# Routing the attention tiles beside attention instead of after it

## The chip, the cores and the metric

The kernel runs on one core of one Trainium2 chip. Its engines are TensorE (PE), VectorE (DVE), ScalarE (ACT), GpSimd (POOL) and SyncE (SP); DMA transfers run on 16 DMA engines and are issued here by SyncE and GpSimd, after the change by ScalarE too. The metric is the device time of one execution in microseconds.

## The reference

For 32 sequences of 256 tokens (D = 128) an attention layer with residual, then four layers of a mixture of experts with residual. Top 2 of 4 experts are chosen for each token by a router; the layers act on u, the normed output of the attention part.

```
x  = x + layernorm(linear_attention(layernorm(x)))     # 16 heads, causal, relu(q), relu(k)
u  = layernorm(x)
for l in range(4):
    logits = u @ router_w[l] + router_b[l]             # top 2 experts, gates from their softmax
    xhat   = normalised u
    expert e: u + gelu((xhat*g[e]+b[e]) @ w1[l,e] + b1[l,e]) @ w2[l,e] + b2[l,e]
    u = gate-weighted sum over the two chosen experts
x  = x + layernorm(u)
```

## The kernel before

The program is two blocks. In the first, attention works on 16 tiles of 512 tokens (`NT`), with x of all tiles in SBUF as `x1`. Each engine runs a `body(t)`, in a hardware loop for the middle tiles. In a body, VectorE masks scores, divides, and takes statistics three times: of x of tile t+1 (`x_stats`), of the projected output of tile t-1 (`o_stats`) and of x1 of tile t-1 (`x1_stats`). For each of the three GpSimd computes the reciprocal deviation (`rstd`: ve, then rs), and VectorE norms with it (`x_norm`, `make_x1`, `make_u`). TensorE transposes the normed xn into `ps_a`, projects to q, k and v, and makes scores and numerators. ScalarE empties PSUM (`evacuate`: xnT, qT, kT, ktok, vx, den) and copies the projection (`copy_o`). `make_u` writes u of all tiles into one SBUF tensor.

SyncE issues in order: x of tile 0, wqkv and wo, the other x tiles one after another, the small parameters, w1, then the zeroing of the two DRAM buffers `regions` (49 transfers each, from a tile `zero`), and then x1 of each tile into the output.

The second block begins with routing the 16 tiles (`for r in range(NT)` on each engine). For a tile, TensorE transposes u (`start_transposes`) and multiplies by the routers of all four layers (`start_logits`); VectorE chooses the two experts (`choose`), finds the gate's argument (`difference`) and, from counts that TensorE sums (`count`), each token's place in the region of its pair of experts (`place`); ScalarE computes the tanh of the gate and copies u into the row; GpSimd writes gates and identity and sends the rows out in four indirect DMAs (`rows_out`). There are two row buffers (`nrow`). Meanwhile w1 and w2 of layer 0 are split into a high and a low part (`split_w1`, `split_w2`) and stored. When all tiles are placed, VectorE makes a table of expert tiles (`table_counts`, `table_tiles`), SyncE stores the biases and loads the first rows (`rows_in`), and the experts' steady loop over 84 tiles runs (`N`).

Of the kernel before, what the change touches and what calls it, by code (L numbers as in the profile page):

```python
# [4 lines left out]
F32 = mybir.dt.float32  # L27
F32R = mybir.dt.float32r
# [41 lines left out]
ZEROS = 49  # L70


def sandwich_kernel(nc, x, wqkv, wo, router_w, router_b, ln_g, ln_b, w1, b1, w2, b2, out):
    ctx = ExitStack()
    with ctx:
# [7 lines left out]
        u = sb("u", [P, NT * TILE])  # L83
# [5 lines left out]
        cs = sb("cs", [P, L * E])  # L89
        rb = sb("rb", [P, L * E])  # L90
        onesf = sb("onesf", [P, P])
# [4 lines left out]
        slot, ones_nb = sb("slot", [P, NB]), sb("ones_nb", [P, NB])  # L96
# [5 lines left out]
        regions = [nc.dram_tensor(f"regions{q}", [ROWS, W], F32).ap() for q in range(2)]  # L102

# [7 lines left out]
        s_regions = sem("regions_zero")  # L111
# [24 lines left out]
        out_t = out.rearrange("(t s) n d -> t (s n) d", t=NT).rearrange("t (b p) d -> t p b d", p=P)  # L136

# [5 lines left out]
        with att:  # L143
# [32 lines left out]
            blank = asb("blank", [P, P])  # L176
            numbers = [asb(f"numbers{n}", [P, n], I32) for n in (NB, CL, NTL)]
# [6 lines left out]
            b1_rows = qx[0]  # L184

# [8 lines left out]
            def _(sp):  # L194
# [4 lines left out]
                with sp.Fori(1, NT) as t:  # L199
                    sp.wait_ge(s_x, t * 16)  # L200
                    sp.dma_start(blocks(x1[:, ds(t * TILE, TILE)]), x_t[ds(t, 1)].rearrange("o p b d -> p (o b) d")).then_inc(s_x, 16)
# [4 lines left out]
                sp.dma_start(rw[:].rearrange("h (l e) -> h l e", l=L), router_w.rearrange("l h e -> h l e")).then_inc(s_small, 16)  # L206
                sp.dma_start(rb[:], router_b.rearrange("l e -> (l e)").partition_broadcast(P)).then_inc(s_small, 16)
# [10 lines left out]
                with sp.Fori(0, NT) as t:  # L218
                    sp.wait_ge(a_x1, t + 1)
                    sp.dma_start(out_t[ds(t, 1)].rearrange("o p b d -> p (o b) d"), blocks(x1[:, ds(t * TILE, TILE)])).then_inc(s_prefill, 16)  # L220
# [3 lines left out]
            def _(pool):  # L224
# [8 lines left out]
                g.memset(onesf[:], 1.0)  # L233
# [23 lines left out]
                with pool.Fori(0, 3 * NT) as n:  # L257
                    rstd(n)

                g.memset(upper[:], 0.0)  # L260
                g.memset(first_row[:], -BIG)
                g.memset(ones6[:], 1.0)
                g.memset(ones_nb[:], 1.0)
                g.memset(ones_b[:], 1.0)
                g.memset(blank[:], 1.0)
                g.iota(numbers[0][:], pattern=[[P, NB]], base=0, channel_multiplier=1)
                g.iota(numbers[1][:], pattern=[[TILE, CL]], base=0, channel_multiplier=0)
                g.iota(numbers[2][:], pattern=[[1, NTL]], base=0, channel_multiplier=0).then_inc(s_c0, 1)
                pool.wait_ge(s_c0, 1)
                g.affine_select(out=blank[:], in_=blank[:], compare_op=ALU.is_ge, fill=0.0, base=-1,  # L270
                                pattern=[[1, P]], channel_multiplier=-1).then_inc(s_c1, 1)
                for q, (e, f) in enumerate(PAIR_CLASSES):
                    c = slice(e * E + f, e * E + f + 1)
                    g.memset(upper[:, c], 1.0)
                    g.memset(class_row[:, q:q + 1], float(TILE + q * TOKENS))
                    g.memset(first_row[:, c], float(TILE + q * TOKENS) - BIG)
                    g.memset(of_class[:, 2, q:q + 1], float(e))
                    g.memset(of_class[:, 3, q:q + 1], float(f))
                g.tensor_copy(slot[:], numbers[0][:])
                g.tensor_copy(thresholds[:], numbers[1][:])  # L280
                g.tensor_copy(tiles[:], numbers[2][:])
                pool.wait_ge(s_c1, 1)
                g.tensor_copy(before[:], blank[:]).then_inc(s_consts, 1)
# [5 lines left out]
            def _(dve):  # L289
# [86 lines left out]
                def make_u(t, n):  # L376
                    dve.wait_ge(a_rs, n + 1)
                    for b in range(NB):
                        last = normed(u[:, ds(t * TILE + b * P, P)], x1[:, ds(t * TILE + b * P, P)], b)
                    last.then_inc(a_u, 1)  # L380

                def body(t, par, prev, nxt, n):
# [27 lines left out]
                    reciprocal(t, 3)  # L410

# [13 lines left out]
                with dve.Fori(1, NT // 2 - 1) as q:  # L425
                    body(q * 2, 0, True, True, q * 6 - 1)
                    body(q * 2 + 1, 1, True, True, q * 6 + 2)
# [15 lines left out]
            def _(act):  # L443
                a = nc.scalar

                def copy_o(t):
                    act.wait_ge(a_o_ps, t + 1)
                    if not isinstance(t, int) or t > 0:
                        act.wait_ge(a_on, t)
                    a.activation(o_sb[:], ps_b[:], ACT.Identity).then_inc(a_o, 1)  # L450

# [29 lines left out]

                evacuate(0, 0)
                evacuate(1, 1)
                copy_o(0)
                evacuate(2, 0)
                copy_o(1)
                evacuate(3, 1)
                with act.Fori(2, NT // 2) as q:
                    copy_o(q * 2 - 2)
                    evacuate(q * 2, 0)  # L490
                    copy_o(q * 2 - 1)
                    evacuate(q * 2 + 1, 1)
                copy_o(NT - 2)
                act.wait_ge(s_cols_ps, 1)
                a.activation(cols[:], ps_a[:, 0:112], ACT.Identity).then_inc(s_cols, 1)
                a.activation(cs[:], ps_a[:, P:P + L * E], ACT.Identity)
                copy_o(NT - 1)
                for l in range(L):
                    act.wait_ge(s_b1rows_ps, l + 1)
                    a.activation(b1_rows[:, l, :], ps_b1[l][:], ACT.Identity).then_inc(s_b1rows, 1)  # L500

            @block.tensor
            def _(pe):
# [5 lines left out]
                def transposes(t):  # L509
                    pe.wait_ge(a_xn, t + 1)  # L510
                    if not isinstance(t, int) or t > 0:
                        pe.wait_ge(a_den, t)
                    for b in range(NB):
                        last = nc.tensor.transpose(ps_a[:, blk(b)], xn[:, blk(b)], ident[:])
                    last.then_inc(a_xT_ps, 1)

# [84 lines left out]
                def body(t, par, prev, nxt):  # L601
                    scores(t, par, 0, not prev)
                    scores(t, par, 1, not prev)
                    if prev:
# [20 lines left out]
                with pe.Fori(1, NT // 2 - 1) as q:  # L625
# [5 lines left out]
                pe.wait_ge(s_small, 6 * 16)  # L631
                pe.wait_ge(a_den, NT)
                nc.tensor.transpose(ps_a[:, 0:112], rows[:], ident[0:112, 0:112])
                mm(ps_a[:, P:P + L * E], onesf[:], rw[:], start=True, stop=True).then_inc(s_cols_ps, 1)
                project(NT - 1)

# [12 lines left out]
                for l in range(L):  # L649
# [3 lines left out]
                    last.then_inc(s_b1_ps, 1)  # L653


        s_ir = sem("identity_router")

        z_uT_ps, z_uT, z_lu_ps, z_lu, z_u = (sem(f"z_{n}") for n in ("uT_psum", "uT", "logits_psum", "logits", "u_copied"))

        s_raw, s_wst, s_whigh, s_wrest = sem("raw_weights_in"), sem("split_weights_out"), sem("weights_high"), sem("weights_rest")  # L660
# [9 lines left out]
        t_id, t_valid, t_link, t_oh, t_nd, t_th, t_gate = (  # L670
            sem(f"t_{n}") for n in ("id", "valid", "chain", "class", "difference", "tanh", "gates"))
        t_cnt, t_pos, t_row, t_base, t_tab = (sem(f"t_{n}") for n in ("counts_psum", "position", "row", "base", "table"))
        s_scat = [sem(f"rows_out{q}") for q in range(2)]
# [3 lines left out]
        w1d = nc.dram_tensor("w1_split", [L, E, P, 2 * F], F32).ap()  # L677
        w2d = nc.dram_tensor("w2_split", [L, E, P, 2 * F], F32).ap()
# [3 lines left out]
        with exp:  # L682
# [9 lines left out]
            wr1, wr2 = esb("wr1", [P, F]), esb("wr2", [P, F])  # L692
            wst1, wst2 = esb("wst1", [P, 2 * F], F32R), esb("wst2", [P, 2 * F], F32R)
# [22 lines left out]
            base = esb("base", [P, CL])  # L716
            ir = esb("ir", [P, D + L * E])
# [18 lines left out]
            def wait(eng, signal, count):  # L736
                if count > 0:
                    eng.wait_ge(signal, count)

            def ps_c(r):  # L740
                return (ps_h[0] if r < NT else ps_q)[:, CNT].rearrange("p (b c) -> p b c", c=CL)
# [681 lines left out]
```

## Time and profile before

| what | value |
|---|---|
| time, median of 3 runs | 1749.76 us (1746.67 to 1753.34) |
| time of the profiled execution | 1748.56 us |
| its span | 1746.5 us |
| mean granted clock of TensorE | 0.933 of full speed |
| busy: PE, DVE, ACT, POOL | 86%, 74%, 70%, 50% |
| DMA moved | 323.96 MB |

The span is the profiled part of the execution. Shares are averages over attention, routing and experts, which have different limits, so they are to be read by stretches of time. SPq in a row is SyncE's queue: its time there is that of issuing a transfer, not of moving it.

### The profile page before, as it was taken

What the parts mean: (1) busy time and instruction counts of PE and PEld (TensorE: products, weight loads), DVE (VectorE), ACT (ScalarE), POOL (GpSimd) and SP (SyncE); (2) the same over time, 40 slices, a digit from 0 to 9 for tenths busy, and PEclk for the clock granted to TensorE, in tenths of its full rate; (3) what the DMA queues carried; (4) which work ended last, traced back from release to release, by engine and by line L of the source; (5) the groups of instructions that cost most, each with busy time, mean ns of one, the idle gap of its engine ahead of it and who ended that gap; (6) DMA issues with size and microseconds to landing.
All of it is one profiled execution on the core that took longest, in us unless ns stands there. A gap on an engine that the chain in (4) does not pass through costs nothing. (4 is left out here: it accounts for less than half of the span.)

```text
span 1746.5 us, 39659 instructions
## 1 busy us (share of the span) xinstructions
PE 1501.3 (86%) x11654; PEld 1179.6 (68%) x11654; DVE 1299.8 (74%) x4048; ACT 1231.0 (70%) x2137; POOL 875.5 (50%) x1434
## 2 busy tenths in 40 slices
PE   7899999843329999989999998999999898888882
PEld 4556655533227888878888887878888787766761
DVE  6989999833337888778888887888888787666662
ACT  4445444211139888878888887888888788999992
POOL 1111111155543555645555554555555457788776
PEclk9999999955559999999999999999999999999996
DMA  3899820012246667656676675567767556766651
GB/s 91 304 404 405 340 65 12 20 62 80 69 146 201 217 209 233 222 182 201 194 223 214 199 239 184 182 195 239 212 210 234 187 192 174 188 180 179 184 137 8
DMA packets 196044, 323.96 MB, mean 185 GB/s; under 512 B 47789, under 2 KB 127999, under 8 KB 195872
## 3 DMA queue, kind: packets, MB, share of 16 engines
q1 hardware_dynamic: 168608, 298.46, 52.0%
q0 software_dynamic: 27264, 23.54, 6.0%
q8 instruction: 67, 1.10, 0.3%
q14 instruction: 105, 0.86, 0.2%
HBM read 218.99 MB, written 108.71 MB: 188 GB/s over the span
## 5 line engine op out<-in xcount | busy, mean ns | idle before, releaser
L1071 DVE TENSOR_TENSOR hl<-hg,hh 128x1024 fp32r<-128x1024 f32 x336 | 409.2, 1221 | 221.1 <-ACT hh L996 221.1
L990 ACT ACTIVATE hg<-ps_h,bb 128x512 f32<-128x512 f32 x672 | 438.4, 684 | 136.2 <-PE ps_h L1343 133.6
L904 POOL DMA_INDIRECT regions<-nrow,posi x316 | 358.0, 1133 | 139.7 <-issue 76.8
L996 ACT ACTIVATE hh<-hg 128x1024 fp32r<-128x1024 f32 x336 | 355.2, 1057 | 2.8
L1341 PE MATMUL ps_h<-xTh,w1b 128*128 128x512 f32 x672 | 288.6, 429 | 2.1 <-DVE xTl L1087 1.4
L1343 PE MATMUL ps_h<-xTh,w1b 128*128 128x512 f32 x672 | 266.8, 397 | 0.0
L1342 PE MATMUL ps_h<-xTl,w1b 128*128 128x512 f32 x672 | 266.3, 396 | 0.0
L1358 PE MATMUL ps_y<-hh,w2b 128*128 128x512 f32 x672 | 266.1, 396 | 0.0
L1356 PE MATMUL ps_y<-hh,w2b 128*128 128x512 f32 x672 | 265.3, 395 | 0.0
L1357 PE MATMUL ps_y<-hl,w2b 128*128 128x512 f32 x672 | 264.6, 394 | 0.0
L1372 PE MATMUL ps_q<-ir,yb 128*128 128x140 f32 (+2 forms) x1008 | 152.8, 284 | 22.5 <-DVE nrow L1108 13.9
L1372 PEld LDWEIGHTS ps_q<-ir,yb 128*128 128x128 f32 x1008 | 134.9, 190 | 48.4 <-issue 23.7
L913 POOL DMA_INDIRECT out_dram<-fin,fidi x84 | 135.0, 1607 | 53.6 <-ACT fin L1008 31.6
L975 ACT ACTIVATE xh<-row,pnmr,prs 128x128 f32<-128x128 f32 x336 | 137.9, 487 | 20.9 <-POOL pnmr L858 20.8
L253 POOL TENSOR_TENSOR ve<-mv,epsc 128x4 f32<-128x4 f32 x48 | 9.6, 201 | 281.6 <-DVE mv L299 281.6
L1343 PEld LDWEIGHTS ps_h<-xTh,w1b 128*128 128x128 f32 x672 | 127.9, 190 | 28.9
L1357 PEld LDWEIGHTS ps_y<-hl,w2b 128*128 128x128 f32 x672 | 127.2, 189 | 29.2
L1356 PEld LDWEIGHTS ps_y<-hh,w2b 128*128 128x128 f32 x672 | 127.2, 189 | 28.6
L1358 PEld LDWEIGHTS ps_y<-hh,w2b 128*128 128x128 f32 x672 | 127.2, 189 | 28.3
L1341 PEld LDWEIGHTS ps_h<-xTh,w1b 128*128 128x128 f32 x672 | 128.4, 191 | 21.1 <-DVE xTl L1087 1.8
L1342 PEld LDWEIGHTS ps_h<-xTl,w1b 128*128 128x128 f32 x672 | 128.6, 191 | 18.4
L893 POOL TENSOR_SCALAR nrow<-th 128x4 f32<-128x4 f32 x79 | 15.6, 198 | 216.0 <-ACT th L961 215.9
(197 smaller groups left out, 2643.2 us busy)
## 6 DMA issues: line engine op xcount, KB each, us to landing
w1b<-w_split SPq DMA_DIRECT2D x168, 512.0 KB, 4.3
w2b<-w_split SPq DMA_DIRECT2D x168, 512.0 KB, 4.2
regions<-zero SPq DMA_DIRECT2D x98, 582.0 KB, 12.8
row<-regions SPq DMA_DIRECT2D x84, 294.0 KB, 4.4
w_split<-wst SPq DMA_DIRECT2D x32, 512.0 KB, 5.2
wr<-in_L_ffn_w_dram SPq DMA_DIRECT2D x32, 256.0 KB, 4.6
regions<-nrow,posi POOLq DMA_INDIRECT x316, 3.0
x<-in_L_attn_x_dram SPq DMA_DIRECT2D x16, 256.0 KB, 2.9
```

The costliest lines, as they stand in the source:

```text
L904: g.indirect_dma_start(out=regions[layer % 2], out_offset=bass.IndirectOffsetOnAxis(ap=posi[r % 2][:, b:b + 1], axis=0), in_=nrow[r % 2][: ...
L975: last = a.activation(xh[:, blk(b)], row[n % ROWBUFS][:, b, 0:D], ACT.Identity, scale=rs[:, b:b + 1], bias=nmr[:, b:b + 1])
L990: a.activation(hg[c // 2 % PAIRS][:, c % 2 * TILE:(c % 2 + 1) * TILE], ps_h[c % BANKS][:], ACT.Gelu, bias=bb[n % 4][k // FC][:, k % FC:k % ...
L996: a.activation(hh[j % PAIRS][:], hg[j % PAIRS][:], ACT.Identity).then_inc(hi, 1)
L1071: v.tensor_tensor(hl[n][:], hg[n][:], hh[n][:].bitcast(F32), ALU.subtract).then_inc(lo, 1)
L1341: mm(o[:], w[:, high], xTh[n % 2][:], start=True, stop=False)
L1342: mm(o[:], w[:, high], xTl[n % 2][:], start=False, stop=False)
L1343: mm(o[:], w[:, low], xTh[n % 2][:], start=False, stop=True).then_inc(s1, 1)
L1356: mm(y[:], w[:, high], hh[j][:, h], start=k % FC == 0, stop=False)
L1357: mm(y[:], w[:, high], hl[j][:, h], start=False, stop=False)
L1358: last = mm(y[:], w[:, low], hh[j][:, h], start=False, stop=k % FC == FC - 1)
L1372: last = mm(o, yb[m % 2][e][:, blk(b)], ir[:, 0:width(m)], start=True, stop=True)
```

## The change

Routing of the attention tiles moves into the first block, tile t-2 in body t. `make_u` writes u straight into one of four row buffers (`arow`). TensorE transposes the row's u (`rows_T`), and multiplies it by the routers and sums the counts (`logits_and_counts`), in `ps_a`; ScalarE empties these and computes the tanh. GpSimd takes over `choose` and `place`, with instructions linked by a semaphore, and sends the rows out between its `rstd`s. Zeroing is issued by ScalarE as 14 transfers (7 zeroing steps in each) before its first `evacuate`. The split of layer 0's weights goes to the ends of bodies 4, 6, 8 and 10, and its loads and stores to SyncE's list. The hardware loops of attention are written out. The second block no longer routes; it begins with the tables and the biases.

```diff
@@ sync, block 1: router and small parameters ahead of x; zeroing gone; weights of layer 0
+                raw_weights(0)
...
-                sp.wait_ge(s_pool0, 1)
-                for q in range(2):
-                    flat = regions[q].rearrange("r w -> (r w)").rearrange("(z p n) -> z p n", z=ZEROS, p=P)
-                    for n in range(ZEROS):
-                        sp.dma_start(flat[n], zero[:]).then_inc(s_regions, 16)
...
+                    g = split_in(t - 1)
+                    if g is not None:
+                        store_weights(g)
+                        if g + 1 < E:
+                            raw_weights(g + 1)
@@ gpsimd, block 1
+                def choose(m):
+
+                    q = arow[m % AROWS]
+                    pool.wait_ge(z_lu, m + 1)
+                    at = D + (L - 1) * E
+                    g.tensor_scalar(q[:, :, ID], slot[:], float(m * TILE), None, ALU.add).then_inc(t_id, 1)
+                    chained(g.tensor_tensor(a_lg[:], q[:, :, at:at + E], over_blocks(rb[:, 0:E]), ALU.add))
+                    link()
...
+                    g.tensor_tensor(a_nd[:], a_pd[:, :, 0], a_pd[:, :, 1], ALU.add).then_inc(t_nd, 1)
+                def place(m):
...
+                    chained(g.tensor_tensor(a_tq[:], counted[:, 0:NB, :], over_blocks(base[:]), ALU.add))
...
+                    g.tensor_scalar(a_posi[m % 2][:], a_posf[:], BIG, None, ALU.add).then_inc(t_row, 1)
...
+                rstd(0)
+                n = 1
+                for t in range(NT + 4):
+                    if t + 1 < NT:
+                        rstd(n)
+                        n += 1
+                    if t == 0:
+                        numbers_and_classes()
+                    if 0 <= t - 4 < NT:
+                        rows_out(t - 4, range(3))
+                    if 0 <= t - 1 < NT:
+                        rstd(n)
+                        n += 1
+                    if 0 <= t - 4 < NT:
+                        rows_out(t - 4, range(3, 4))
+                    if 0 <= t - 1 < NT:
+                        rstd(n)
+                        n += 1
+                    if 0 <= t - 3 < NT:
+                        place(t - 3)
+                    if 0 <= t - 2 < NT:
+                        choose(t - 2)
+                pool.wait_ge(s_regions[1], ZEROS // ZBATCH * 16)
+                for q in range(2):
+                    pool.wait_ge(s_scat[q], NT // 2 * NB * 16)
@@ vector, block 1
                     for b in range(NB):
-                        last = normed(u[:, ds(t * TILE + b * P, P)], x1[:, ds(t * TILE + b * P, P)], b)
+                        last = normed(arow[t % AROWS][:, b, 0:D], x1[:, ds(t * TILE + b * P, P)], b)
...
                     reciprocal(t, 3)
+                    if split_in(t) is not None:
+                        split(split_in(t))
@@ scalar, block 1
+                    rows_T(t)
...
+                        copy_o(t - 1)
+                    logits_and_counts(t)
+                    if t + 1 < NT:
+                        evacuate(t + 1, (t + 1) % 2)
+                    if split_in(t) is not None:
+                        split(split_in(t))
...
+                act.wait_ge(s_pool0, 1)
+                for q in range(2):
+                    flat = regions[q].rearrange("r w -> (r w)").rearrange("(y z p n) -> y p z n", y=ZEROS // ZBATCH, z=ZBATCH, p=P)
+                    for y in range(ZEROS // ZBATCH):
+                        a.dma_start(flat[y], zero[:].unsqueeze(1).to_broadcast([P, ZBATCH, zero.shape[-1]])).then_inc(s_regions[q], 16)
                 evacuate(0, 0)
@@ tensor, block 1: body(t)
+                    if t >= 2:
+                        rows_T(t)
                     if prev:
                         project(t - 1)
                     numerator(t, par, 0, not prev)
+                    logits_and_counts(t)
                     scores(t, par, 2, False)
                     if nxt:
                         transposes(t + 1)
@@ block 2: the loops over r in range(NT) are gone on all engines
```

## Rows read from the trace of the kernel before

**Rows 1.** The page's first line: span of the profiled execution.
```profile
span 1746.5 us, 39659 instructions
```
**Rows 2.** Busy time by stretches: stretch, length, engines, clock, DMA share, GB/s.
```profile
240.00:260.00 20.00, 18.49 (x342) 11.97 (x342) 18.92 (x57) 9.19 (x19) 3.64 (x6) 1.00 0.04 13
352.00:492.00 140.00, 49.45 (x272) 42.57 (x272) 49.63 (x243) 24.20 (x56) 74.48 (x125) 0.50 0.21 71
```
**Rows 3.** Timeline, GpSimd, routing: start, us, engine, line, operation [idle before <-releaser].
```profile
370.74 1.08 POOL L904 DMA_INDIRECT regions<-nrow,posi  x1 [0.80 <-POOL posi L898]
...
497.44 0.97 POOL L904 DMA_INDIRECT regions<-nrow,posi  x1 [0.30 <-issue]
498.72 0.97 POOL L904 DMA_INDIRECT regions<-nrow,posi  x1 [0.30 <-issue]
```
**Rows 4.** Timeline, VectorE and SyncE's queue, end of the routing stage.
```profile
489.00 0.74 DVE L1216 SCALAR_TENSOR_TENSOR wst<-wr,cols,wst 128x512 fp32r<-128x512 f32 x1
490.26 0.34 DVE L1165 TENSOR_TENSOR num<-base,first_row 128x3 f32<-128x3 f32 x3
...
494.71 0.20 DVE L1207 CAST tabi<-tabf 128x84 int32<-128x84 f32 x1
...
503.30 4.12 SPq L813 DMA_DIRECT2D row<-regions  x4
```
**Rows 5.** Timeline, SyncE's queue, attention.
```profile
56.00 154.68 SPq L217 DMA_DIRECT2D regions<-zero  x98
211.05 134.82 SPq L220 DMA_DIRECT2D out_dram<-x  x16
```
**Rows 6.** Line 217, the zeroing transfers: time of an issue, and to landing.
```profile
L217 SPq DMA_DIRECT2D regions<-zero x98: 332/1318/4249, 56.0 to 209.2; - x98
...
DMA to landing us min/median/max: 5.4/12.8/19.1
```
**Rows 7.** DMA traffic of the stretch from 60 to 215 us.
```profile
DMA packets 15772, 60.91 MB, mean 393 GB/s; under 512 B 1623, under 2 KB 2103, under 8 KB 15762
```
**Rows 8.** Timeline, ScalarE, start of the kernel and one tile.
```profile
9.07 0.60 ACT L459 ACTIVATE xnT<-ps_a 128x512 f32<-128x512 f32 x1 [7.00 <-PE ps_a L514]
...
241.96 0.69 ACT L480 ACTIVATE den<-ps_a,epsc 128x512 f32<-128x512 f32 x1 [3.97 <-DVE rec L334]
```
**Rows 9.** Timeline, GpSimd and VectorE, start of the kernel and end of attention.
```profile
2.69 0.11 POOL L234 MEMSET order<- 128x16 f32 x1
...
348.26 1.16 DVE L286 TENSOR_SCALAR u<-x,mv,rs 128x128 f32<-128x128 f32 x4 [1.41 <-POOL rs L255]
...
351.35 0.29 POOL L919 COPY ir<-ident 128x128 f32<-128x128 f32 x1 [0.35 <-POOLq L143]
```
**Rows 10.** Timeline, GpSimd, one tile of attention.
```profile
249.96 0.20 POOL L253 TENSOR_TENSOR ve<-mv,epsc 128x4 f32<-128x4 f32 x1 [4.54 <-DVE mv L299]
...
255.31 0.20 POOL L253 TENSOR_TENSOR ve<-mv,epsc 128x4 f32<-128x4 f32 x1 [4.06 <-DVE mv L299]
255.59 1.01 POOL L255 TENSOR_TENSOR rs<-ve,half 128x4 f32<-128x4 f32 x1
264.20 0.20 POOL L253 TENSOR_TENSOR ve<-mv,epsc 128x4 f32<-128x4 f32 x1 [7.60 <-DVE mv L299]
```
**Rows 11.** Timeline, VectorE and GpSimd, experts.
```profile
541.89 1.24 DVE L1071 TENSOR_TENSOR hl<-hg,hh 128x1024 fp32r<-128x1024 f32 x1 [1.01 <-ACT hh L996]
...
542.03 1.28 POOL L877 TENSOR_SCALAR valid<-slot,tabf 128x4 f32<-128x4 f32 x1
```
**Rows 12.** Timeline, VectorE, one tile of attention.
```profile
245.45 1.11 DVE L286 TENSOR_SCALAR xn<-x,mv,rs 128x128 f32 x4 [0.19 <-POOL rs L255]
...
256.33 1.26 DVE L322 TENSOR_TENSOR_SCAN cumk<-ones,kT 128x256 f32<-128x256 f32 x2
257.63 0.69 DVE L325 TENSOR_TENSOR qcumk<-qT,cumk 128x512 f32<-128x512 f32 x1
```
**Rows 13.** DMA issues: line, KB each, median us from issue to landing.
```profile
biases<-bst SPq DMA_DIRECT2D x1, 40.0 KB, 9.7
```

More of the change, by code:

```diff
@@ L110, in sandwich_kernel @@
         s_w1all = sem("w1_all_in")
-        s_regions = sem("regions_zero")
+        s_regions = [sem(f"regions_zero{q}") for q in range(2)]
+        s_router = sem("router_in")
+        s_raw, s_wst, s_whigh, s_wrest = sem("raw_weights_in"), sem("split_weights_out"), sem("weights_high"), sem("weights_rest")
+        z_uT_ps, z_uT, z_lu_ps, z_lu, z_cnt = (sem(f"z_{n}") for n in ("uT_psum", "uT", "logits_psum", "logits", "counts"))
+        z_pool = sem("z_chain")
+        t_id, t_valid, t_link, t_oh, t_nd, t_th, t_gate = (
+            sem(f"t_{n}") for n in ("id", "valid", "chain", "class", "difference", "tanh", "gates"))
+        t_cnt, t_pos, t_row, t_base, t_tab = (sem(f"t_{n}") for n in ("counts_psum", "position", "row", "base", "table"))
+        s_scat = [sem(f"rows_out{q}") for q in range(2)]
         s_c0, s_c1, s_consts = sem("constants_blank"), sem("constants_numbers"), sem("routing_constants")
@@ L255, in rstd @@
                     g.tensor_tensor(rs[:], ve[:], half[:], ALU.pow).then_inc(a_rs, 1)
[L257 to L283, printed above, removed]
+                def numbers_and_classes():
+                    g.memset(upper[:], 0.0)
+                    g.memset(first_row[:], -BIG)
+                    g.memset(ones6[:], 1.0)
+                    g.memset(ones_b[:], 1.0)
+                    g.memset(blank[:], 1.0)
+                    g.memset(a_oh[:, NB, :], 0.0)
+                    g.iota(numbers[0][:], pattern=[[P, NB]], base=0, channel_multiplier=1)
+                    g.iota(numbers[1][:], pattern=[[TILE, CL]], base=0, channel_multiplier=0)
+                    g.iota(numbers[2][:], pattern=[[1, NTL]], base=0, channel_multiplier=0).then_inc(s_c0, 1)
+                    pool.wait_ge(s_c0, 1)
+                    g.affine_select(out=blank[:], in_=blank[:], compare_op=ALU.is_ge, fill=0.0, base=-1,
+                                    pattern=[[1, P]], channel_multiplier=-1).then_inc(s_c1, 1)
+                    for q, (e, f) in enumerate(PAIR_CLASSES):
+                        c = slice(e * E + f, e * E + f + 1)
+                        g.memset(upper[:, c], 1.0)
+                        g.memset(class_row[:, q:q + 1], float(TILE + q * TOKENS))
+                        g.memset(first_row[:, c], float(TILE + q * TOKENS) - BIG)
+                        g.memset(of_class[:, 2, q:q + 1], float(e))
+                        g.memset(of_class[:, 3, q:q + 1], float(f))
+                    g.tensor_copy(slot[:], numbers[0][:])
+                    g.tensor_copy(thresholds[:], numbers[1][:])
+                    g.tensor_copy(tiles[:], numbers[2][:])
+                    pool.wait_ge(s_router, 32)
+                    g.tensor_copy(ir[:, 0:D], ident[:])
+                    for l in range(L):
+                        g.tensor_copy(ir[:, D + (L - 1 - l) * E:D + (L - l) * E], rw[:, l * E:(l + 1) * E])
+                    pool.wait_ge(s_c1, 1)
+                    g.tensor_copy(before[:], blank[:]).then_inc(s_consts, 1)
+                    pool.wait_ge(s_consts, 1)
+                    g.tensor_copy(base[:], first_row[:]).then_inc(s_consts, 1)
@@ new lines, in _, with chained, link, over_blocks @@
+                links = [0]
+                def chained(op):
+                    op.then_inc(z_pool, 1)
+                    links[0] += 1
+                def link():
+                    pool.wait_ge(z_pool, links[0])
+                def over_blocks(ap):
+                    return ap.unsqueeze(1).to_broadcast([P, NB, ap.shape[-1]])
+                def folded(values):
+                    for n in (8, 4, 2):
+                        link()
+                        chained(g.tensor_tensor(values[:, :, 0:n], values[:, :, 0:n], values[:, :, n:2 * n], ALU.add))
+                    link()
@@ new lines, in rows_out @@
+                def rows_out(m, some):
+                    if some[0] == 0:
+                        pool.wait_ge(t_row, m + 1)
+                        pool.wait_ge(t_gate, m + 1)
+                        pool.wait_ge(t_id, m + 1)
+                        if m == 0:
+                            pool.wait_ge(s_regions[0], ZEROS // ZBATCH * 16)
+                    for b in some:
+                        g.indirect_dma_start(out=regions[0], out_offset=bass.IndirectOffsetOnAxis(ap=a_posi[m % 2][:, b:b + 1], axis=0),
+                                             in_=arow[m % AROWS][:, b, :], in_offset=None,
+                                             bounds_check=ROWS - 1, oob_is_err=False).then_inc(s_scat[m % 2], 16)
@@ L424, in _ @@
                 body(1, 1, True, True, 2)
-                with dve.Fori(1, NT // 2 - 1) as q:
+                for q in range(1, NT // 2 - 1):
                     body(q * 2, 0, True, True, q * 6 - 1)
@@ L480, in evacuate @@
                     a.activation(den[:], ps_a[:], ACT.Identity, bias=epsc[:, 0:1]).then_inc(a_den, 1)
-                evacuate(0, 0)
[L483 to L497, printed above, removed]
+                act.wait_ge(s_pool0, 1)
[3 more added lines that the diff above has]
+                        a.dma_start(flat[y], zero[:].unsqueeze(1).to_broadcast([P, ZBATCH, zero.shape[-1]])).then_inc(s_regions[q], 16)
+                evacuate(0, 0)
+                for t in range(NT + 1):
+                    body(t)
                 for l in range(L):
@@ L500, in _ @@
                     a.activation(b1_rows[:, l, :], ps_b1[l][:], ACT.Identity).then_inc(s_b1rows, 1)
+                for t in range(NT + 1, NT + 3):
+                    body(t)
             @block.tensor
@@ L515, in transposes, with columns, rows_T, logits_and_counts @@
                     last.then_inc(a_xT_ps, 1)
+                def columns():
+                    pe.wait_ge(s_small, 4 * 16)
+                    pe.wait_ge(a_den, 2)
+                    nc.tensor.transpose(ps_a[:, 0:112], rows[:], ident[0:112, 0:112]).then_inc(s_cols_ps, 1)
+                def rows_T(t):
+                    pe.wait_ge(a_den, min(t + 1, NT))
+                    pe.wait_ge(a_u, t - 1)
+                    wait(pe, z_lu, t - 2)
+                    wait(pe, z_cnt, t - 3)
+                    for b in range(NB):
+                        last = nc.tensor.transpose(ps_a[:, blk(b)], arow[(t - 2) % AROWS][:, b, 0:D], ident[:])
+                    last.then_inc(z_uT_ps, 1)
+                def logits_and_counts(t):
+                    if 0 <= t - 2 < NT:
+                        pe.wait_ge(s_consts, 1)
+                        pe.wait_ge(z_uT, t - 1)
+                        for b in range(NB):
+                            last = mm(ps_a[:, b * L * E:(b + 1) * L * E], uT[:, blk(b)], ir[:, D:], start=True, stop=True)
+                        last.then_inc(z_lu_ps, 1)
+                    if 0 <= t - 3 < NT:
+                        pe.wait_ge(t_oh, t - 2)
+                        if t - 2 >= NT:
+                            pe.wait_ge(z_lu, NT)
+                        o = ps_a[:, COUNTS].rearrange("p (b c) -> p b c", c=CL)
+                        mm(o, before[:], a_oh[:], start=True, stop=False, skip_group_check=True)
+                        for b in range(NB):
+                            last = mm(o[:, b + 1:, :], ones_b[:], a_oh[:, b, :].unsqueeze(1).to_broadcast([P, NB - b, CL]),
+                                      start=False, stop=b == NB - 1, skip_group_check=True)
+                        last.then_inc(t_cnt, 1)
                 def qk(t):
@@ L624, in _ @@
                 body(1, 1, True, True)
-                with pe.Fori(1, NT // 2 - 1) as q:
+                for q in range(1, NT // 2 - 1):
                     body(q * 2, 0, True, True)
@@ L629, in _ @@
                 body(NT - 1, 1, True, False)
[L631 to L634, printed above, removed]
+                rows_T(NT)
                 project(NT - 1)
+                logits_and_counts(NT)
                 pe.wait_ge(s_cols, 1)
@@ L734, in blk, with ps_c @@
                 return slice(b * P, (b + 1) * P)
[L736 to L741, printed above, removed]
+            def ps_c():
+                return ps_q[:, CNT].rearrange("p (b c) -> p b c", c=CL)
             def width(m):
```

238 lines of the change are left out of this document (136 added, 102 removed).

## The prediction

> **What bounds the kernel now.** I read the span first, then busy time by stretches, and then each engine's timeline where a stretch changes character. The span is 1746.5 us [rows 1]; the profiled execution is timed at 1748.56 us, so 2.06 us lie outside the span, and it stands 0.07% under the median of 1749.76. The sum below is made against 1748.56. Three runs reach from 1746.67 to 1753.34, so 0.5% (about 9 us) is about what a measurement can tell from no change.
>
> By stretches [rows 2] the kernel has three parts. In attention VectorE is busy 18.92 of 20 us and TensorE 18.49, GpSimd 3.64. In the routing stage from 352 to 492 us nobody is full: GpSimd is busy 74 of 140 us, TensorE 49 at half its clock. The reader is to see a stage of waits: for each tile four row scatters leave GpSimd 1.3 us apart, after a wait [rows 3], and the next tile waits for their landing. The experts begin when SyncE loads the first rows, at 503.30 [rows 4]. What follows (1746.5 - 503.3 = 1243.2 us) the change leaves alone. So everything is decided by when that first load of rows can be issued.
>
> Before attention there is one more thing to see, on SyncE's queue. The 98 zeroing transfers hold that engine from 56.00 for 154.68 us [rows 5]. One issue takes a median of 1.3 us and up to 4.2 [rows 6], though the shortest takes 0.33, while the 16 DMA engines move 393 GB/s [rows 7]. The issue is long because the queue has no room: a transfer lands 12.8 us after its issue, which at 393 GB/s is 5.0 MB already queued. SyncE can afford this; its next work, writing x1 out, simply comes late, at 211.05 [rows 5].
>
> **Zeroing moved to ScalarE's queue.** The same bytes (98 x 582 KB = 57.0 MB) become 14 transfers of 4.07 MB, issued by ScalarE ahead of `evacuate(0)`. Behind them in ScalarE's order stands all of attention: TensorE waits for xnT, which ScalarE writes first at 9.07 [rows 8], and VectorE waits for TensorE. The nearest row says that an engine whose queue is full is held until the queue drains. ScalarE is free when the last transfer fits in: 57.0 MB less the 5.0 MB that may still be queued is 52 MB, at 393 GB/s 132 us, from about 3 us on (GpSimd's memsets come first, rows 9). SyncE now loads x and weights in the same time, some 9 MB (4.2 of x, 4.2 of w1, 0.5 of raw weights), which would be 23 us if all of it came first; I take half. ScalarE is then free at 3 + 132 + 11, about 145 us. Lower bound: the queue takes two whole transfers (8.1 MB) and nothing competes, 3 + 49/0.393 = 128. Upper bound: the whole 154.68 of the old issue, plus 23, is 180. From 9.07 to 145 attention starts 136 us late; nothing else is waiting to fill that time.
>
> The Trainium skill (DMA: Bandwidth & Descriptors, "Issuing engines are not separate DMA queues") says that issuing from another engine saves only the sequencer's time to initiate a DMA, usually small beside the DMA. By that the 14 issues would cost ScalarE a few us in all and the first rival below would be the outcome. The trace does not agree for transfers that fill the queue: 154.68 us of SyncE went into issuing [rows 5].
>
> **Routing moved beside attention.** Removed: the stage from the last u, written by 349.42 [rows 9], to 503.30. Added to attention, by engine:
>
> GpSimd. A tile's `choose` and `place` are 25 small instructions, 19 of which wait for the one before. No row shows 64-element two-input work on GpSimd. The shortest linked step is ve to rs, 0.28 us from start to start [rows 10]; a 128-element copy takes 0.29 [rows 9], with the 0.08 of a link 0.37. I take 0.35 for the linked ones and 0.2 for six others: 6.65 + 1.2 = 7.9 us. The lower bound is 19 x 0.28 + 6 x 0.16 = 6.3. To this comes being held by VectorE: where `hl` (two SBUF inputs) runs 1.24 us, a GpSimd instruction of four elements lasts 1.28 [rows 11]. In the window where `choose` falls, VectorE runs the cumk scan (1.26, some 1.0 of it inside) and qcumk (0.69), both of two SBUF inputs [rows 12]. I add 1.6 and take 9.5 us; the upper bound takes 0.37 a link and 3 us held, 11.5.
> The window: rs of x1 ends at 256.60, and the next x's mv calls GpSimd at 264.20 [rows 10], which is 7.6 us. Four scatters (5.2 us, rows 3) go into the two other gaps, of 4.54 and 4.06 us of idle time [rows 10], which have room. GpSimd executes in order, so an rstd that stands behind `choose` is 9.5 - 7.6, about 2 us late. xn waits for it already now, by 0.19 us [rows 12], so VectorE loses all of it. This happens for some 11 tiles (those with both parts and a later x): 22 us; bounds 0 and 44.
>
> TensorE. Routing's transposes, logits and counts took 49.45 us for 16 tiles at the lower clock level [rows 2], 3.1 a tile, so 1.6 to 2 at the full one, into 1.5 us of idle time per tile. At most 0.5 too much, and it runs beside the 2 us of GpSimd: nothing. If GpSimd were no bound, it would cost 0 to 6 us. ScalarE adds four short copies to 9.19 busy us of 20: nothing.
>
> VectorE, weight splits. In four tiles `split` is queued ahead of the next `divide`. It waits for ScalarE, which comes to its two 0.60 us copies only after den [rows 8]: 0.69 + 1.2 + 0.2 is 2.1 us, then two operations of 0.74 [rows 4]. Of these 3.5 us GpSimd's lateness covers 2.0, so 4 x 1.5 = 6 us; alone 14.
>
> **The tail.** After the last u GpSimd still owes, in order: place and choose (7.9, unheld now), four scatters (5.2), place and choose (7.9), scatters (5.2), place (2.9), a wait of 0.8 [rows 3], scatters (5.2). That is 35, starting 1.2 us before u ends, and a landing of 3.6 (from the end of the last scatter to 503.30, rows 3, 4): 37.5 us. The next block begins 1.9 us later, as now [rows 9]. Then SyncE stores the biases, which landed 9.7 us after issue [rows 13], before it may load rows; formerly routing hid that. With ScalarE's copies 10.5 us. The tables (490.26 to 494.91, rows 4) are shorter and hide behind it. Together 37.5 + 1.9 + 10.5, about 50 us.
>
> **Sum.** First rows are loaded at 145 + (349.42 - 9.07 = 340.3) + 22 + 6 + 50 = 563 us, instead of 503: 60 us later. 1748.56 + 60 = 1809 us. With all low bounds 128, 0, 14 (the splits uncovered): 1748.56 + (128 + 340 + 14 + 50 - 503) = 1778; with the high ones 180, 44 and 0: 1748.56 + (180 + 340 + 44 + 50 - 503) = 1860. The tail may be off by 12 either way.
>
> **Rivals.** (1) ScalarE is not held: the issue hands each big transfer over and returns. For it: 14 issues are few, and the shortest issue is 0.33 us [rows 6]. Against it: out-writes of another kind also stood in SyncE's queue until 211 us. Attention starts at 9, rows are loaded at 427 us, and the time is 1748.56 - 76 = 1672 us. The point of change is ScalarE free at 145 - 60 = 85 us; earlier is faster than before. This is the case on the other side.
> (2) ScalarE is held, but a deeper queue or larger transfers let it go between 65 and 125 us: 1728 to 1789 us.
> (3) GpSimd fits its window and only the splits show: 145 + 340 + 14 + 50, so 1794. Or GpSimd is held at every step and becomes the bound of attention, 4 us a tile: 1825. Both are of the likeliest kind; only the size differs.
> The Trainium skill (GPSIMD Engine Reference, 3.1) gives about 2.6 cycles an element for two inputs at 1.2 GHz, an estimate of 0.14 us more for 64 elements; a linked step would be 0.42 and the sum some 15 us higher.
>
> **How the numbers follow.** Held to the end 0.75 (1809; its own range 1770 to 1872), held for less 0.08, not held 0.15, anything else 0.02. The range 1738 to 1875 takes the first with its bounds and most of the second, about 0.8; it leaves out the case that ScalarE isn't held. Slower: 0.73 of the first and 0.06 of the second, 0.79. Within 0.5%: 0.04. Faster: 0.17.
>
> **What would show it.** Right: ScalarE's timeline has 14 transfers from about 3 us to 145 us and its first xnT only then; the other engines are empty so long; in attention xn waits for rs about 2 us a tile; scatters run inside attention; after the last u some 50 us pass to the first load of rows, the last 10 of them for the biases. Wrong: xnT at about 9 us with zeroing running beside attention, as in rival 1; or attention tiles well over 24 us, with GpSimd late beyond its bounds.

## The result, and the profile after

The change makes the kernel slower: 1797.43 us (median of 4, 1796.41 to 1802.08) beside 1748.22 for the kernel before in the same comparison, a ratio of 1.0282 (95% interval 1.0252 to 1.0311). Forecast were 1809 us and slower. The profiled execution was timed at 1797.55 us; its span is 49.3 us over that of [rows 1].

```profile
span 1795.8 us, 38770 instructions
```

Start with ScalarE's timeline (start, us, engine, line, operation), which answers to [rows 8].

```profile
2.69 124.76 ACTq L674 DMA_DIRECT2D regions<-zero  x14
...
127.48 1.28 ACT L647 ACT_TABLE_LOAD   x1 [127.48 <-issue]
128.77 0.60 ACT L647 ACTIVATE xnT<-ps_a 128x512 f32<-128x512 f32 x1
```

ScalarE does nothing but issue for 124.76 us; the first xnT is written at 128.77 instead of 9.07. The view of line 674 gives the issues' times (shortest, median, longest in ns), and DMA traffic of the stretch from 2.7 to 127.45 us says what moved meanwhile, by queue (packets, MB, share of 16 engines; q10 is ScalarE's, q1 SyncE's). They answer to [rows 6, 7].

```profile
L674 ACTq DMA_DIRECT2D regions<-zero x14: 456/10338/19182, 2.7 to 117.1; - x14
...
DMA to landing us min/median/max: 12.6/36.3/44.5
```

```profile
DMA packets 17272, 51.58 MB, mean 413 GB/s; under 512 B 1120, under 2 KB 6857, under 8 KB 17272
...
q10 hardware_dynamic: 10591, 48.49, 94.3%
q1 hardware_dynamic: 6681, 3.09, 8.5%
```

An issue has a median of 10.3 us, close to the 10.1 us that its 4.17 MB take at 413 GB/s: the issues go at the pace at which the queue drains. Busy time by stretches (columns as in [rows 2]) shows what that does to the others.

```profile
20.00:40.00 20.00, 0.00 (x0) 0.00 (x0) 0.00 (x0) 0.00 (x0) 0.00 (x0) 1.00 1.03 415
...
200.00:220.00 20.00, 19.63 (x360) 13.14 (x359) 18.98 (x57) 10.03 (x24) 9.98 (x28) 1.00 0.05 15
240.00:260.00 20.00, 16.45 (x189) 10.54 (x188) 14.90 (x47) 5.52 (x13) 12.01 (x26) 0.66 0.10 30
```

From 20 to 120 us every engine is empty. From 200 to 220 attention runs as before, VectorE at 18.98 of 20, with GpSimd now at 9.98. From 240 to 260 lies a tile with a weight split, and TensorE's granted clock there is 0.66 in the mean: in stretches of 4 us it is 0.50, the lower of its two levels (1.2 of 2.4 GHz), from 244 to 256 us, after TensorE had stood 2.31 us for VectorE's yT at 240.4. VectorE's timeline shows the start of the tile before, and then that tile:

```profile
222.15 1.12 DVE L415 TENSOR_SCALAR xn<-x,mv,rs 128x128 f32<-128x128 f32 x4 [1.19 <-POOL rs L273]
...
240.60 0.75 DVE L516 SCALAR_TENSOR_TENSOR wst<-wr,cols,wst 128x512 fp32r<-128x512 f32 x1 [1.94 <-ACT wst L624]
241.27 0.74 DVE L518 TENSOR_TENSOR wst<-wr,wst 128x512 fp32r<-128x512 f32 x1
...
245.42 1.27 DVE L415 TENSOR_SCALAR xn<-x,mv,rs 128x128 f32<-128x128 f32 x4 [0.26 <-POOL rs L273]
...
258.87 1.29 DVE L472 TENSOR_TENSOR sc<-ps_s,causal 128x512 f32<-128x512 f32 x2 [2.64 <-PE ps_s L782]
```

xn waits 1.19 us for GpSimd. The split (`wst`) waits 1.94 us for ScalarE; after it xn hardly waits, but 15 us later the mask (`sc`) waits 2.64 for TensorE, which had run at the lower clock level since 244. The sums of VectorE's waits in attention (total us, times, longest), after and then before:

```profile
DVE sc L472 <- PE ps_s L782: 11.6, 9, 2.6
DVE wst L516 <- ACT wst L624: 7.8, 4, 1.9
DVE xn L415 <- POOL rs L273: 7.1, 13, 1.2
DVE on L415 <- POOL rs L273: 6.5, 2, 5.8
```

```profile
DVE sc L343 <- PE ps_s L562: 4.6, 3, 2.0
...
DVE xn L286 <- POOL rs L255: 2.6, 13, 0.2
...
DVE on L286 <- POOL rs L255: 1.4, 1, 1.4
```

At the end (VectorE, GpSimd and SyncE's queue, answering to [rows 3, 4]; `on` is the normed projection, `arow` the row buffer that u is written to):

```profile
496.96 1.30 DVE L415 TENSOR_SCALAR on<-o_sb,mv,rs 128x128 f32<-128x128 f32 x4 [5.83 <-POOL rs L273]
...
501.97 1.39 DVE L415 TENSOR_SCALAR arow<-x,mv,rs 128x128 f32<-128x128 f32 x4 [1.44 <-POOL rs L273]
```

```profile
535.90 0.97 POOL L384 DMA_INDIRECT regions<-arow,a_posi  x1 [0.30 <-issue]
544.18 0.11 POOL L1122 MEMSET oh<- 128x16 bf16 x1 [7.30 <-POOLq L137]
```

```profile
544.59 0.37 SPq L1025 DMA_DIRECT2D biases<-bst  x1
551.30 4.74 SPq L1021 DMA_DIRECT2D row<-regions  x4
```

So the first rows are loaded at 551.30, 48.0 us later than in [rows 4]. That is 119.7 from ScalarE's late start (128.77 - 9.07), 34.2 from longer attention (128.77 to the end of the last u at 503.36 is 374.59, before it was 340.35), and -105.9 from what routing took after the last u (47.9 us, before 153.9). Behind the first load the rest takes 1244.5 us, before 1243.2.

### The profile page after: what moved, and what is told of

It reads as the page before. It is cut to its first block and busy times, and to the rows that moved or that the text cites. A ratio compares the mean times of both kernels' runs of the same rounds, so it can differ in the third digit from the quotient of the medians.

```text
span 1795.8 us, 38770 instructions
## 1 busy us (share of the span) xinstructions
PE 1494.1 (83%) x11652; PEld 1172.7 (65%) x11652; DVE 1260.8 (70%) x3823; ACT 1227.1 (68%) x2152; POOL 977.7 (54%) x1772
## 5 line engine op out<-in xcount | busy, mean ns | idle before, releaser
L1107 POOL DMA_INDIRECT regions<-nrow,posi x252 | 296.1, 1175 | 112.0 <-issue 62.2
L1505 PEld LDWEIGHTS ps_y<-hl,w2b 128*128 128x128 f32 x672 | 127.3, 189 | 29.2
L1504 PEld LDWEIGHTS ps_y<-hh,w2b 128*128 128x128 f32 x672 | 127.4, 190 | 28.5
L741 PE MATMUL ps_b<-xnT,wqkv_sb 128*128 128x512 f32 x32 | 20.9, 738 | 120.5 <-ACT xnT L647 120.5
## 6 DMA issues: line engine op xcount, KB each, us to landing
regions<-zero ACTq DMA_DIRECT2D x14, 4074.0 KB, 36.3
x<-in_L_attn_x_dram SPq DMA_DIRECT2D x16, 256.0 KB, 11.3
```

Of the source, the lines that this page charges most:

```text
L1107: g.indirect_dma_start(out=regions[layer % 2], out_offset=bass.IndirectOffsetOnAxis(ap=posi[r % 2][:, b:b + 1], axis=0), in_=nrow[r % 2][: ...
L1504: mm(y[:], w[:, high], hh[j][:, h], start=k % FC == 0, stop=False)
L1505: mm(y[:], w[:, high], hl[j][:, h], start=False, stop=False)
```

## The experiments

All times are medians, ratios are to the kernel before, run beside each.

**Zeroing alone, in the kernel before.** Is it this edit that makes attention late, or another one?

```diff
...
-                    for n in range(ZEROS):                       # SyncE
-                        sp.dma_start(flat[n], zero[:]).then_inc(s_regions, 16)
...
+                act.wait_ge(s_pool0, 1)                          # ScalarE, 7 transfers for each region
...
+                        a.dma_start(flat[y], zero[:].unsqueeze(1).to_broadcast([P, ZBATCH, zero.shape[-1]])).then_inc(s_regions, 16)
                 evacuate(0, 0)
```

> The kernel before with one part of the change alone: zeroing as 14 transfers of 4.07 MB from ScalarE ahead of its first evacuate, nothing of it from SyncE. Theory (ScalarE is held until its queue has room for the last transfer): first xnT at 125 to 130 us instead of 9.07, nothing hides it, so 1748 + 120 = 1868 us (1855 to 1880). Rival (the late start after the change comes from another edit, such as the loads now ahead on SyncE or the written-out loops): xnT at about 9 us and 1748 us, within 1%.

```profile
2.83 124.70 ACTq L481 DMA_DIRECT2D regions<-zero  x14
...
128.85 0.60 ACT L454 ACTIVATE xnT<-ps_a 128x512 f32<-128x512 f32 x1
```

1864.72 us, ratio 1.0648 (1.0626 to 1.0669): 112.7 us over the kernel before beside it (116.6 by the spans of the two profiled executions), for 119.8 us of later xnT. The edit by itself does it.

**Smaller transfers.** `ZEROS, ZBATCH = 49, 1` in the changed kernel.

> The changed kernel with the zeroing in 98 transfers of 582 KB instead of 14 of 4.07 MB, still all from ScalarE ahead of evacuate(0). Theory (bytes through the queue set the hold): ScalarE free at 127 us again, within 10, so 1797 us within 10. Rival (the number of issues sets it, 1.58 us for each as SyncE's 98 took before): ScalarE free at about 157, so 1827 us.

```profile
2.69 138.27 ACTq L674 DMA_DIRECT2D regions<-zero  x98
```

1811.57 us, ratio 1.0342 (1.0321 to 1.0364), and xnT at 142.29: between the two, so neither expectation holds. One issue takes 1.41 us on average, so it isn't the 1.58 of before; but ScalarE was freed 13.5 us later than with 14 transfers, with 53.00 MB through its queue instead of 48.49.

**Two transfers of 28.5 MB.** `ZEROS, ZBATCH = 49, 49`.

> The changed kernel with zeroing in 2 transfers of 28.5 MB, both from ScalarE ahead of evacuate(0). In the changed kernel the first two of 14 transfers were issued in 1.1 us and the third was held. Theory A (the queue has room for two whole transfers of any size): ScalarE free before 5 us, first xnT at 9, 1683 us within 15. Theory B (one whole transfer in hand and 5 MB in the rings): free when all but 5 MB of the first is through, at about 62 us, 1732 us within 10. Theory C (room for 9.9 MB): free at 127 us, 1797 us.

ScalarE's timeline, and the traffic of its queue until it was free:

```profile
2.70 61.65 ACTq L674 DMA_DIRECT2D regions<-zero  x2
```

```profile
q10 hardware_dynamic: 5078, 23.64, 92.9%
```

1733.62 us, ratio 0.9902 (0.9884 to 0.992): theory B, to 2 us. The zeroed regions are 2 x 49664 rows of 588 bytes, 58.4 MB. When ScalarE was freed there was left of them 58.4 - 23.6 = 34.8 MB with two transfers (29.2 + 5.6), 58.4 - 48.5 = 9.9 with 14 (4.2 + 5.7), and 5.4 with 98. So the queue takes some 5 MB, and, with large transfers, one whole transfer more. That accounts for the three; why it is so isn't shown, and as the data packets have 4656 bytes in all three, nor is whether the queue counts bytes or packets.

**Half ahead.** Region 0's 7 transfers ahead of `evacuate(0)`, region 1's one after each of bodies 3 to 9 (`zero_next(1 if 3 <= t < 10 else 0)` after `body(t)`; `zero_next(n)` issues the next n of the 14).

> The changed kernel with region 0's 7 transfers ahead of evacuate(0) and region 1's one in each of bodies 3 to 9. Theory (hold in proportion to the bytes over the queue's room): ScalarE free 28.5 MB / 0.414 MB per us = 69 us earlier than the 127.5 of the change, at 58.6, so 1797.4 - 69 = 1728 us (1718 to 1742): on the other side of the break-even at 85 us. Rival (the queue takes the first transfers freely and only the later ones are held): ScalarE free before 20 us and about 1690.

```profile
2.69 50.66 ACTq L632 DMA_DIRECT2D regions<-zero  x7
```

1722.03 us, ratio 0.9842 (0.9818 to 0.9867), as the theory has it; xnT at 54.68. From here to the changed kernel xnT comes 74.1 us later and the time is 75.4 us longer, one for one. A time of 1750 us lies 28 us above this one, at an xnT of 82 and a ScalarE free at 81 us; the prediction had the break-even at 85.

**Spread.** One transfer ahead of `evacuate(0)`, one after it, and then:

```diff
                     logits_and_counts(t)
+                    zero_next(1 if t in (1, 2) else 0)
...
+                    zero_next(1 if t < 10 else 0)                # after body(t)
```

> The changed kernel with the same 14 transfers from ScalarE, but one ahead of evacuate(0), one after it and the others one or two in each of bodies 0 to 9, so that the queue has room. Theory (only the hold is lost time): first xnT at 9 to 12 us, first rows 119.7 us earlier, 1797.4 - 119.7 = 1678 us (1668 to 1700, as zeroing beside attention may cost a few us), faster than before. Rival (the 57 MB have to be written before rows can go out, or slow attention's own transfers, so the wait only moves): over 1740 us, with GpSimd waiting for the zeroed regions or VectorE for x.

The same 14 transfers, by line and in ScalarE's timeline:

```profile
L632 ACTq DMA_DIRECT2D regions<-zero x14: 378/378/455, 2.7 to 249.4; - x14
```

```profile
8.90 0.60 ACT L657 ACTIVATE xnT<-ps_a 128x512 f32<-128x512 f32 x1 [4.44 <-PE ps_a L709]
```

1683.42 us, ratio 0.9608 (0.9581 to 0.9635). An issue now takes 0.38 us at the median and 0.46 at most: the bytes are the same, the hold is gone, and with it 114.0 us. The first rows come at 437.7. Attention with zeroing beside it is 6 us longer than in the changed kernel; TensorE's timeline and stretches of 4 us show some of it:

```profile
88.48 0.67 PE L810 MATMUL ps_num<-sc,vx 64*32 64x64 f32 x37 [2.24 <-issue]
```

```profile
84.00:88.00 4.00, 2.24 (x43) 1.39 (x36) 3.86 (x12) 0.82 (x4) 1.21 (x2) 1.00 1.04 408
88.00:92.00 4.00, 3.52 (x41) 1.48 (x40) 3.02 (x14) 0.60 (x1) 0.50 (x2) 0.70 1.03 417
```

TensorE stands for 2.24 us, the profile names nothing that it waits for, and its granted clock falls afterwards, to 0.70 over the next 4 us. The last section comes back to this.

**Zeroing back on SyncE.** The other edits stay; the 98 transfers go after the x and w1 loads, ahead of the stores of x1.

> The changed kernel with zeroing back on SyncE: 98 transfers after the x and w1 loads and ahead of x1's stores, as before the change; ScalarE issues none. Theory (whoever issues is held for some 155 us, and what stands behind it is late): attention starts at 9 us, but the first rows wait for region 0 until about 145 instead of 95 us, which holds GpSimd and so VectorE's xn for some 50 us, and the weights of the second split stand behind the stores, some 40 us more; 1683 + 90 = 1770 us (1740 to 1795). Rival (SyncE hides the zeroing as it did before): 1683 us, within 15.

GpSimd's and ScalarE's timelines:

```profile
143.60 1.26 POOL L389 DMA_INDIRECT regions<-arow,a_posi  x1 [39.06 <-issue]
```

```profile
231.35 0.72 ACT L628 ACTIVATE wst<-wr,cols 128x512 fp32r<-128x512 f32 x1 [22.76 <-DMA wr<-in_L_ffn_w_dram]
```

1739.91 us, ratio 0.9953 (0.9935 to 0.9971), at the lower edge of what was expected: 57.5 us under the changed kernel, and 56.5 over spread zeroing. SyncE issues for 154.23 us; the scatters stand 39 us before the first of them, whose line waits for the zeroed region, and the second split 23 us for weights queued behind the stores. Both waits are the expected ones, each smaller. So zeroing on SyncE doesn't come free either once rows go out during attention: held is whoever issues it all at once.

**Place earlier on GpSimd**, on the spread zeroing:

```diff
+                    if 0 <= t - 3 < NT:
+                        place(t - 3)
                     if 0 <= t - 1 < NT:
                         rstd(n)
                         n += 1
-                    if 0 <= t - 3 < NT:
-                        place(t - 3)
```

and for the last tile (t = NT) the four scatters behind the rstd of o.

> On the spread zeroing (1683.4 us): GpSimd's place goes ahead of the rstd of x1, which is needed only at the body's end, and for the last tile the rstd of o goes ahead of the three scatters. Theory (GpSimd was late for xn by choose and place in one window): xn's wait of 0.8 to 1.2 us falls to 0.2 to 0.3 in some 10 tiles, and the 5.8 us wait of the last tile's on to about 1.4: 10 x 0.9 + 4.4 = 13 us less, 1670 us (1662 to 1676). Rival (xn's wait is not what VectorE loses, because TensorE comes next): within 4 us of 1683 but for the last tile, 1679.

```profile
377.74 1.29 DVE L415 TENSOR_SCALAR on<-o_sb,mv,rs 128x128 f32<-128x128 f32 x4 [1.43 <-POOL rs L273]
...
387.19 1.12 DVE L415 TENSOR_SCALAR arow<-x,mv,rs 128x128 f32<-128x128 f32 x4 [5.89 <-POOL rs L273]
```

1677.83 us (ratio 0.9588, 0.957 to 0.9606): 5.6 us instead of 13. xn's waits did fall to 0.26 us each, but with spread zeroing they had summed to 5.8 us only, where the expectation had some 10 tiles of 1 us: in a tile that stalls elsewhere GpSimd has more time. By the two profiled executions, whose spans lie 3.6 us apart, attention became 1.4 us shorter and the stretch from the last u to the first rows 2.9, as a `place` that stood behind the last rstd now stands ahead of it. So the time is outside the theory's range and close to the rival's 1679, and most of what was gained is not xn's. And the wait of the last `on`, gone from 5.8 to 1.43, turned up at the last u: the scatters now stood ahead of its rstd.

**Splits later**, on the spread zeroing: VectorE's two split instructions go into body t+1, one after `reciprocal(t, 0)`, one after `reciprocal(t, 1)`.

> On the spread zeroing (1683.4 us): VectorE's two split instructions go from the end of bodies 4, 6, 8, 10 into the next body, behind the first and the second reciprocal, when ScalarE's halves have long been there. Theory (the wait for ScalarE, 1.94 us four times, and the lower clock after it are lost time): the waits go, TensorE's clock stays at its upper level there, 4 x (1.94 + 1.5) = 14 us less, 1670 us (1664 to 1676). Rival (the two instructions of 0.75 us cost as much in any place and TensorE's queue absorbs the wait): 1680 to 1684.

The sums of VectorE's waits in attention, with spread zeroing and then with later splits:

```profile
DVE sc L472 <- PE ps_s L791: 16.0, 11, 2.7
DVE wst L516 <- ACT wst L624: 7.8, 4, 1.9
...
DVE xn L415 <- POOL rs L273: 5.8, 13, 1.2
```

```profile
DVE xn L415 <- POOL rs L273: 10.2, 12, 1.2
...
DVE sc L472 <- PE ps_s L795: 6.4, 5, 2.4
```

1672.09 us (ratio 0.956, 0.9544 to 0.9576): 11.3 us. The 7.8 us for ScalarE are gone and 9.6 us for TensorE with them (8.1 us of waits stood within 20 us behind a split; the rest belongs to stalls like the one above, which changed too), while xn waits 4.4 us longer: GpSimd's lateness had been hidden behind the splits, as the prediction said. TensorE's granted clock from 128 to 148 us, around the first split, is 1.00 here and 0.74 with spread zeroing.

**Both**, with the last tile's four scatters behind both of its rstds.

> Spread zeroing, place early and split later together, and for the last tile the four scatters behind both rstds. Theory (each removes a loss of its own): 1683.4 - 5.6 (place) - 11.3 (split) - 5.9 (the last u's wait for the scatters, seen with place early) = 1661 us (1655 to 1666). Rival (the losses overlap, since a tile with a split did not lose GpSimd's lateness): 1668 us or more.

```profile
DVE sc L474 <- PE ps_s L797: 10.6, 5, 2.6
...
DVE xn L417 <- POOL rs L273: 3.4, 13, 0.3
```

1661.41 us (1660.01 to 1664.49), ratio 0.9502 (0.9486 to 0.9518), where the theory had 1661 and the rival 1668 or more: 22.0 us less than spread zeroing alone and the fastest version here, 86.8 us below the kernel before and 136 below the changed one.

**Zeroing earlier and thinner**, on that: region 0's 7 transfers by the end of body 1, region 1 in 49 of 582 KB, four or five after each of bodies 3 to 14.

> The combined kernel with region 0's 7 transfers earlier (two ahead of evacuate(0), two after it, two after body 0, one after body 1) and region 1 in 49 transfers of 582 KB, four or five in each of bodies 3 to 14. Theory (TensorE's stalls of 1.1 to 2.4 us that no wait explains come only while the DMA engines are full beside attention, and each brings a stretch at the lower clock): from 80 us on DMA is below full, the stalls at about 88 and 111 us are gone, and 2 x (2.2 + 1.5) = 7 us go: 1654 us (1648 to 1659). Rival (the stalls belong to these tiles whatever DMA does, and 49 more issues cost ScalarE): 1661 us or more, with the stalls in the same places.

TensorE's timeline:

```profile
46.77 1.01 PE L723 MATMUL ps_a<-ident,xn 128*128 128x128 f32 x4 [2.15 <-issue]
...
72.94 0.82 PE L824 MATMUL ps_num<-sc,vx 64*32 64x64 f32 x52 [2.10 <-issue]
```

1671.22 us (ratio 0.956, 0.953 to 0.9591), 9.8 us more than the version before it: neither expectation holds, since the time rose and the stalls didn't stay in place. The stall at 90.7 us went and the one at 114.9 fell from 2.36 to 0.81 us, but others came at 46.8 and 72.9, where DMA is now full, one of 1.44 us at 138.3 stayed, and two came that end at 311.2 and 332.9. There the mean DMA share over 20 us is 0.4, but stretches of 1 and 2 us (columns as in [rows 2]) show that it comes in bursts:

```profile
306.00:308.00 2.00, 2.00 (x21) 1.23 (x21) 2.00 (x4) 0.44 (x3) 1.39 (x3) 1.00 1.03 400
...
310.00:311.00 1.00, 0.00 (x0) 0.00 (x0) 1.00 (x3) 0.00 (x0) 0.85 (x1) 1.00 0.04 10
```

Four transfers issued together fill DMA until 308, and TensorE stands still just behind them. The edit made more bursts, not a thinner stream, so the loss that it was to remove is still there, and what the 49 issues themselves cost ScalarE can't be told from it.

## Why the prediction was right

**What decides.** The prediction took [rows 5, 6] as a rule: an engine that issues more than its queue has room for is held until the queue drains. The edit alone in the kernel before costs 113 us, and spreading the same bytes gives 114 back. The rule is shown, and rival 1 (not held) falls for these transfers. The Trainium skill (DMA: Bandwidth & Descriptors, "Issuing engines are not separate DMA queues") calls the time to initiate a DMA usually small beside the DMA itself. The traces agree where the queue has room (0.38 us, beside 14.6 to landing), and do not where it hasn't (10.3 us at the median, beside 36.3).

**The sizes.** Taken from the profiled execution, the forecast came out 11 us high. ScalarE was free at 127.5 instead of 145, half a us under the lower bound. The term furthest off is the room: 5.0 MB were assumed, 9.9 were left when ScalarE was freed, because a whole large transfer is taken beyond the 5; the lower bound had reckoned with two whole ones, 8.1 MB. That is 12.5 us. The bandwidth was 413 GB/s over the stretch, where 393 was taken from another (6.4 us), and of SyncE's traffic only 3.1 MB fell into it, where half of 9 was assumed (3.6). Against that, the bytes were 58.4 MB and not 57.0, as a KB of the page is 1024 bytes (3.6), and the activation table takes 1.3 us after the hold. xnT came at 128.8, 16 us before the 145 of the sum. (Two bounds of the prediction add up otherwise: the low sum less the tail's 12 is 1766, not 1770, and GpSimd's upper case 11.2 us, not 11.5. Nothing here hangs on them.)

**Attention** lost 34.2 us instead of 28, and the parts were other than forecast, so that the sum came this close is partly luck. GpSimd's lateness was to be the largest term, 22 us; VectorE's xn waits only 4.5 us more than before in sum. `choose` and `place` take 7.7 to 7.85 us after attention (forecast 7.9), and beside VectorE mostly 8.7 in tiles without a split and 9.4 in tiles with one (forecast 9.5). Of the 11 tiles named, four show the wait: xn stands 1.2 us there, which goes with 8.7 less the window of 7.6. In the other seven, the four with a split and three behind one, VectorE was itself late and xn waits 0.26 us. The splits were put at 6 us, 14 uncovered. They show 7.8 of waits and 4 x 1.49 = 6.0 of work, and 7.0 more of waits for TensorE, at least part of it at the lower clock after the splits. That clock is what the step lacked: a wait of 2 us in a full pipeline was priced as 2 us. Not foreseen were the 5.1 us of the last tile, where three scatters stand ahead of an rstd; the prediction had placed the scatters in gaps that the last tile doesn't have. These sum to 30.4 of the 34.2 us. Moving the splits gave 11.3 us back and so bore this out; moving `place` gave 5.6, most of it behind the last u and with the last tile's wait only moved on, and the two together, with that wait gone, 22.0.

**The tail** came to 47.9 us where 50 were forecast, the largest difference being that the rows are loaded 6.7 us after the issue of the biases, not 9.7.

**The rivals.** Rival 2, larger transfers that let ScalarE go early, came true when it was made: with two of 28.5 MB it was free at 64 us, at the edge of the 65 to 125 named, for 1734. The part of the change that was worth having is worth more than the prediction's rival of 1672: with the hold and three smaller losses removed, 1661.

## What to carry to other kernels

An issue costs its few tenths of a microsecond only while the queue has room; in a profile, compare the shortest with the median issue, and price a burst of transfers by its bytes over the bandwidth if anything stands behind them on that engine. If the bytes aren't needed at once, issue them a transfer at a time between the engine's own work. When work is put into gaps of an in-order engine, look at the first and the last pass of the loop, where the gaps differ, and expect a wait removed in one place to appear at the next instruction that was hidden behind it.

## What the hardware showed beyond that

Issuing fewer, larger transfers freed the issuing engine sooner for the same bytes: at 141.0 us with 98, 127.5 with 14, 64.4 with 2.

TensorE stood still for 1.1 to 2.6 us, waiting for nothing that the profile shows, two to five times in each kernel with zeroing beside the changed attention, and once in the kernel before (2.53 us, ending at 87.99, while SyncE zeroed). In the two kernels whose 14 transfers go ahead of attention there was no such stall of over 1 us in attention. The stalls moved when the zeroing was moved, and two of them stand just behind a burst of full DMA.

The traces show what goes with them. The profile has a queue q8 of the kind `instruction`, whose packets have 16 KB. DMA traffic from 86 to 88.5 us with spread zeroing, the stretch of the stall that ends at 88.48, has one:

```profile
q8 instruction: 1, 0.02, 2.5%
```

In each of the 22 stalls of over 1 us in attention, in all kernels, such a packet starts between 1.4 us before and 0.1 us after the stall's start, and the stall ends 1.2 to 1.6 us after the packet's end. In the attention of the changed kernel, at a mean DMA share of 0.23, 46 such packets pass without a stall of this kind. So TensorE probably stands for its own next instructions, which come late when DMA is full. That is argued from the times: no run here separates it.
